# A mixture-of-experts block loop and its tail, put in another order

## The reference

```python
x = layernorm(x + dilated_attention(x))              # no weights
x = layernorm(x + cross_attention(x, ctx, Wq, Wkv, Wout))
# the part that this change touches: 32 experts, 8 of them for each of 2048 tokens
probs = softmax(x @ gate_w); w, sel = top_k(probs, 8); w = w / sum(w)
# tokens are gathered per expert (at most C = 1024 each), then per expert:
y = (silu(xg @ w_gate) * (xg @ w_up)) @ w_down       # 256 -> 96 -> 256
out[token] += w * y                                  # 8 results per token
x = layernorm(x + out)
```

## Time and profile before

| what | value |
|---|---|
| time, median of 3 runs | 707.81 us (704.06 to 709.6) |
| the profiled execution | 708.35 us, of which 706.4 us lie between its first and last instruction |
| granted clock of PE, mean over the span | 0.933 of full speed |
| busy share of the span | PE 80%, PEld 58%, POOL 55%, DVE 53%, ACT 47% |
| first stage and tables | to about 370 us |
| block loop | 377 to 645 us |
| tail | 648 to 706.4 us |

### The profile page before, as it was taken

How to read it: one execution, slowest core, us unless ns; L and a number is a source line. 1 busy time by engine, 2 the same in 40 slices (tenths; PEclk the granted TensorE clock), 3 DMA queues, 4 the chain that set the end, 5 groups by cost and what they waited for, 6 DMA issues and landing times.

```text
span 706.4 us, 17346 instructions
## 1 busy us (share of the span) xinstructions
PE 563.3 (80%) x5098; PEld 413.0 (58%) x5099; DVE 375.4 (53%) x1533; ACT 330.2 (47%) x1204; POOL 389.7 (55%) x596
## 2 busy tenths in 40 slices
PE   3768878787888778888509899989989998894995
PEld 3445444455545444554207777777877776774884
DVE  1438666667666666676333455445445544453553
ACT  2436444445554545455304555555555554553012
POOL 5353455454455655554564666666766665664532
PEclk9989999999999999999658999999999999998998
DMA  9599999821112211211235555455555554545994
GB/s 188 177 287 264 356 369 339 287 74 46 59 61 74 74 60 70 75 58 65 87 130 164 160 156 165 148 164 161 167 159 159 154 157 124 164 150 173 425 417 140
DMA packets 80540, 118.51 MB, mean 168 GB/s; under 512 B 13043, under 2 KB 70269, under 8 KB 78464
## 3 DMA queue, kind: packets, MB, share of 16 engines
q1 hardware_dynamic: 63808, 78.63, 37.0%
q0 software_dynamic: 13824, 37.78, 14.5%
q10 hardware_dynamic: 2880, 1.74, 0.8%
HBM read 56.07 MB, written 66.22 MB: 173 GB/s over the span
## 4 chain that ended last, share of the span: by engine, by line
issue 38%; PE 33%; SPq 15%; DMA 6%; POOL 2%; ACT 2%; DVE 2%; ACTq 1%; another core or an unknown queue 0%; POOLq 0%; DVEq 0%
PE bank L792 14%; PE bank L808 10%; SPq L337 8%; PE bank L784 5%; PE bank L802 3%; DMA out<-fin 3%; SPq L333 2%; DMA wall<-results 2%; SPq L332 2%; SPq L331 1%; ACTq L299 1%; ACT th L954 1%; DVE tg L1228 1%; ACT fin L983 1%; DVE hg L1231 1%
## 5 line engine op out<-in xcount | busy, mean ns | idle before, releaser
L552 POOL DMA_INDIRECT results<-ys,wcol x152 | 150.5, 990 | 25.6 <-POOL pscrap L541 19.6
L528 POOL DMA_INDIRECT queues<-x,xidx x128 | 129.4, 1011 | 37.1 <-issue 37.1
L792 PE MATMUL bank<-wall,xtT 128*128 x616 | 128.1, 331 | 1.0 <-issue 0.8
L869 ACT ACTIVATE pr<-bank,nmax 128x128 f32<-128x128 f32 x256 | 90.9, 371 | 30.1 <-DVE nmax L1021 29.7
L1228 DVE SCALAR_TENSOR_TENSOR tg<-th,bank 128x96 f32<-128x96 f32 x154 | 39.0, 253 | 116.3 <-ACT th L954 88.8
L792 PEld LDWEIGHTS bank<-wall,xtT 128*128 128x128 f32 x616 | 99.2, 195 | 2.0 <-issue 2.0
L960 ACT ACTIVATE ys<-bank,wcol 128x256 f32<-128x256 f32 x152 | 71.9, 473 | 55.6 <-PE bank L808 42.6
L808 PE MATMUL bank<-wall,hT 96*128 x304 | 95.1, 394 | 0.0
L784 PE MATMUL bank<-ident,xt 128*128 128x128 f32 x310 | 63.8, 288 | 23.4 <-DMA xt<-queues 12.1
L784 PEld LDWEIGHTS bank<-ident,xt 128*128 128x128 f32 x310 | 59.1, 198 | 38.2 <-issue 18.9
L875 ACT COPY prT<-bank 128x512 f32<-128x512 f32 x64 | 38.5, 601 | 88.5 <-PE bank L607 88.5
(11 more groups left out here) (186 smaller groups left out, 917.7 us busy)
## 6 DMA issues: line engine op xcount, KB each, us to landing
xt<-queues SPq DMA_DIRECT2D x162, 160.0 KB
results<-zeros SPq DMA_DIRECT2D x16, 1024.0 KB
wall<-results SPq DMA_DIRECT2D x16, 1024.0 KB, 13.6
queues<-zeros SPq DMA_DIRECT2D x2, 1760.0 KB
wall<-in_L_ffn_w_gate SPq DMA_DIRECT2D x4, 768.0 KB
wall<-in_L_ffn_w_up SPq DMA_DIRECT2D x4, 768.0 KB
wall<-in_L_ffn_w_down SPq DMA_DIRECT2D x4, 768.0 KB
results<-ys,wcol POOLq DMA_INDIRECT x152
```

What stands on the lines that cost most here:

```text
L528: pool.indirect_dma_start(xg, bass.IndirectOffsetOnAxis(ap=xidx[:, par, k:k + 1], axis=0), x2[:, par, :], None, bounds_check=last_row, oob ...
L552: pool.indirect_dma_start(yr, bass.IndirectOffsetOnAxis(ap=wcol[:, u, 1:2], axis=0), ys[:, u, :], None, bounds_check=last_y, oob_is_err=Fa ...
L792: ins = pe.matmul(bank[2 + u % 2][:, 0:2 * INTER].rearrange("p (g i) -> p g i", g=2), xtT[:, u % 2, kk, :], wall[:, bass.ds(e, GU)].rearrange(
L869: ins = act.activation(pr[:, g % 2, q, :], pS[g % 2][:, q * P:(q + 1) * P], ACT.Exp, bias=nmax[:, 4 * g + q:4 * g + q + 1], accum_out=den[ ...
```

## The change

Three things are put in another order, all by hand.

**The loop.** In step t PE now does the row turn of block t+5 first, then the down product of t, the turn of `hg` of t+2, and gate and up of t+4. ACT does the row copy of t+5, y of t, tanh of t+4; DVE `h_T` of t+2, `weights` of t+3, `gate` of t+4. Blocks are turned five steps ahead of their down product instead of three. Two steps more of turning and of gate and up run past the end of the list. As the second turning product of a step no longer stands behind anything that implies it, it waits by itself until ACT has read the bank that the next down product writes (`y` of block t-2).

**PE's registers.** The eight table entries per round are fetched four at a time, behind steps 1 and 5 of a round, into registers that are kept over the branch; at the end of a round eight register moves put them into place.

**The tail.** SP issues all its loads first and then its stores. A group of batches is stored by four DMAs in all, straight from a buffer for every batch (the first eight in `ys`, the others in `kP`, both free by then), so ACT waits for no earlier store. The groups are 4, 4, 4, 3 and 1.

```diff
-LEAD = UN - 2
+LEAD_G = UN
+LEAD_W = UN - 3
+LEAD_X = UN - 2
+HALF = UN // 2
-LAST = (4, 4, 4, 2, 2)
+LAST = (4, 4, 4, 3, 1)
...
+        def finished(b0, b1):
+
+            if b1 <= UN:
+                return ys[:, b0:b1, :]
+            return kP[:, :, :, :, :].rearrange("p a m q k -> p (a m q k)").rearrange(
+                "p (b d) -> p b d", d=D)[:, b0 - UN:b1 - UN, :]
...
-                eng.dma_start(out[b, t0:t0 + DIL * (GR - 1) + 1:DIL, :],
-                              fin[GR * g:GR * (g + 1), b % 4, :]).then_inc(stored[b % 4], 16)
+                eng.dma_start(out[b0:b1, t0:t0 + DIL * (GR - 1) + 1:DIL, :].rearrange("b i d -> i b d"),
+                              finished(b0, b1)[GR * g:GR * (g + 1), :, :]).then_inc(stored, 16)
...
-            for b in range(NB):
-                if b + YB < NB:
-                    sp.wait_ge(peC, b + 1)
-                    load_results(b + YB)
-                sp.wait_ge(actC, b + 1)
-                store(sp, b, 2, NG)
+            for b in range(YB, NB):
+                sp.wait_ge(peC, b - YB + 1)
+                load_results(b)
+            for n, end in zip(LAST, itertools.accumulate(LAST)):
+                sp.wait_ge(actC, end)
+                store(sp, end - n, end, 2, NG)
...
+                    if kk == 1 and not isinstance(t, int):
+                        pe.wait_ge(actF["y"], t - 4)
...
             with pe.Fori(0, rounds) as j:
-                e = neighbours(ET.PE, tab_g[0:1, bass.ds(j * UN + UN, UN)], (NE - 1) * WX)
                 for u in range(UN):
                     t = j * UN + u
-                    block_T(t + 3, u + 3, j)
-                    gu(t + 2, u, e[u])
-                    turn_h(t + 1, u + 1)
-                    down(t, u, e[u - 2] if u >= 2 else carried[u])
-                for u in range(2):
-                    pe.reg_mov(last_two[u], e[UN - 2 + u])
+                    block_T(t + 5, u + 5, j)
+                    down(t, u, down_e[u] if u < HALF else gate_e[u - HALF])
+                    turn_h(t + 2, u + 2)
+                    gu(t + 4, u + 4, gate_e[u] if u < HALF else later_e[u - HALF])
+                    if u == 1:
+                        later_e = experts_of(j * UN + (LEAD_G + UN))
+                    if u == UN - 3:
+                        coming_e = experts_of(j * UN + (LEAD_G + UN + HALF))
+                for r, v in zip(down_regs + gate_regs, later_e + coming_e):
+                    pe.reg_mov(r, v)
...
-                    block_T(t + 3, u + 3)
-                    tanh(t + 2, u)
+                    block_T(t + 5, u + 5)
                     y(t, u)
+                    tanh(t + 4, u + 4)
...
                 for i in range(n):
-                    if b >= 4:
-                        act.wait_ge(stored[b % 4], 16 * NG * (b // 4))
...
-                    act.wait_ge(actC, b)
-                    store(act, b - 1, 0, 2)
+                act.wait_ge(actC, b)
+                store(act, b - n, b, 0, 2)
...
-                columns = neighbours(ET.DVE, tab_w[0:1, bass.ds(j * UN + UN, UN)], D + NE - 1)
                 for u in range(UN):
                     t = j * UN + u
-                    weights(t + 2, u + 2, j, columns[u])
-                    gate(t + 2, u)
-                    h_T(t + 1, u + 1)
+                    h_T(t + 2, u + 2)
+                    if u == 0:
+                        columns = neighbours(ET.DVE, tab_w[0:1, bass.ds(j * UN + UN, UN)], D + NE - 1)
+                    weights(t + 3, u + 3, j, columns[u])
+                    gate(t + 4, u + 4)
```

More of the change, by code:

```diff
@@ L208, in build @@
         ys = sb("ys", [P, UN, D])
-        fin = sb("fin", [P, 4, D])
         pair_y = sb("pair_y", [P, 4, 2 * D])
@@ L260, in build @@
         y_in = [sem(f"y_in{k}") for k in range(YB)]
-        stored = [sem(f"stored{k}") for k in range(4)]
+        stored = sem("stored")
         gate_v = w_gate.rearrange("e (p k) i -> p e (k i)", k=2)
@@ L293, in neighbours, with store @@
                 skip_runtime_bounds_check_because="the tables hold rows and columns of these arrays only")[1]
-        def store(eng, b, first, last):
+        def finished(b0, b1):
[3 more added lines that the diff above has]
+                "p (b d) -> p b d", d=D)[:, b0 - UN:b1 - UN, :]
+        def store(eng, b0, b1, first, last):
             for g in range(first, last):
                 t0 = first_token(g)
-                eng.dma_start(out[b, t0:t0 + DIL * (GR - 1) + 1:DIL, :],
-                              fin[GR * g:GR * (g + 1), b % 4, :]).then_inc(stored[b % 4], 16)
+                eng.dma_start(out[b0:b1, t0:t0 + DIL * (GR - 1) + 1:DIL, :].rearrange("b i d -> i b d"),
+                              finished(b0, b1)[GR * g:GR * (g + 1), :, :]).then_inc(stored, 16)
         def combined(k):
@@ L348, in rows_of @@
                 return neighbours(ET.SP, tab_x[0:1, bass.ds(first, UN)], XG_ROWS - P)
-            first, second = rows_of(0)[LEAD:], rows_of(UN)
+            first, second = rows_of(0)[LEAD_X:], rows_of(UN)
             for k in range(2):
@@ L809, in down, with kept_registers @@
                           start=True, stop=True).then_inc(peF["y"], 1)
[L811 to L817, removed]
+            def kept_registers(name, values):
+                regs = [nc.alloc_register(ET.PE, f"{name}{k}") for k in range(HALF)]
+                for r, v in zip(regs, values):
+                    pe.reg_mov(r, v)
+                return regs, [bass.RuntimeValue.of_register_unchecked(r).with_bounds(min_val=0, max_val=(NE - 1) * WX)
+                              for r in regs]
@@ L818, in _, with experts_of @@
+            def experts_of(first):
+                return neighbours(ET.PE, tab_g[0:1, bass.ds(first, HALF)], (NE - 1) * WX)
+            down_regs, down_e = kept_registers("down_e", experts_of(LEAD_G))
+            gate_regs, gate_e = kept_registers("gate_e", experts_of(LEAD_G + HALF))
+            block_T(0, 0, 0)
+            block_T(1, 1, 0)
+            gu(0, 0, down_e[0])
+            block_T(2, 2, 0)
+            gu(1, 1, down_e[1])
+            block_T(3, 3, 0)
             turn_h(0, 0)
+            gu(2, 2, down_e[2])
@@ L965, in _ @@
                 act.copy(spare[0:1, k:k + 1], tab_n[0:1, 0:1]).then_inc(actF["y"], 1)
-            for t in range(3):
-                block_T(t, t)
-            for t in range(2):
+            block_T(0, 0)
+            for t in range(4):
+                block_T(t + 1, t + 1)
                 tanh(t, t)
@@ L1196, in tables @@
                 dve.wait_ge(s, H("fe"))
-                for tab, first, times, plus in ((tab_g, LEAD, WX, 0), (tab_w, LEAD, 1, D)):
+                for tab, first, times, plus in ((tab_g, LEAD_G, WX, 0), (tab_w, LEAD_W, 1, D)):
                     dve.tensor_scalar(tab[0:1, first:first + TAB], tab_f[0:1, 0, :], float(times), float(plus),
@@ L1237, in h_T @@
                 dve.tensor_copy(hT[:, u % 2, :], bank[4 + u % 2][0:INTER, 0:P]).then_inc(dveF["hT"], 1)
-            for t, column in zip((0, 1), neighbours(ET.DVE, tab_w[0:1, 0:UN], D + NE - 1)[LEAD:]):
+            for t, column in zip(range(3), neighbours(ET.DVE, tab_w[0:1, LEAD_W:LEAD_W + 3], D + NE - 1)):
                 weights(t, t, 0, column)
+            gate(0, 0)
+            gate(1, 1)
             for t in range(2):
-                gate(t, t)
-            h_T(0, 0)
+                h_T(t, t)
+                gate(t + 2, t + 2)
             with dve.Fori(0, rounds) as j:
-                columns = neighbours(ET.DVE, tab_w[0:1, bass.ds(j * UN + UN, UN)], D + NE - 1)
                 for u in range(UN):
                     t = j * UN + u
-                    weights(t + 2, u + 2, j, columns[u])
-                    gate(t + 2, u)
-                    h_T(t + 1, u + 1)
+                    h_T(t + 2, u + 2)
[3 more added lines that the diff above has]
+                    gate(t + 4, u + 4)
             for u in range(UN):
```

17 lines of the change are left out of this document (10 added, 7 removed).

## The result

The changed kernel takes 704.91 us in the median of 20 runs (698.83 to 709.32), the kernel before 711.12 in 20 runs (704.06 to 720.84). The ratio is 0.9917, with an interval of 0.9891 to 0.9944. So the change gains 0.8%, some 6 us; 42 were forecast, and 705 lies outside the range of 653 to 689. The profiled execution took 698.83 us, of which 697.0 lie between its first and last instruction.

A forecast was written before the change was run, and what follows sets the result against it. PE was taken to bound the loop, busy 240.0 of 268.0 us. The sum 708.35 - 22.3 (hold-ups) - 16.9 (fetches) - 2.3 (tail) = 666.9 gave a forecast of 666 us against 707.8, range 653 to 689.

The forecast's parts named there:

- So PE sets the pace: Loop: PE, busy 240.0 of 268.0 us, is the limit; 152 blocks at 1.42 are 215.8 us, 52.2 too many.
- the gain of 22.3 us from the hold-ups: Loop: 31.3 us of PE's waits (25.0 for `hg`, 6.3 short gaps) become between 0 and 14.3, 9 taken.
- I expect the late results to stay ... then costs 1.38 - 0.88: Loop: gate-and-up results still reach ACT 1.38 us late, slack becomes 0.88; 0.50 plus a 0.16 restart gap remains each time.
- the 0.66 of distance: Loop: from gate and up to the turn of `hg`, 2.07 us before and 2.73 after, so 0.66 more.
- The fetch: PE's register fetch at each round's head: 18.9 us lost before, 2 taken after, gain 16.9; four entries near 0.55 us.
- The wait for `y`: PE's wait in the loop for `y` of block t-2, issued two steps before: answered in time, so 0.
- the loads: Block loads in the loop: 8.5 us of lead against a landing of 2.1 us, so 0.
- POOL's own time: POOL in the loop: needs 1.36 us a block against PE's step of 1.42, so it isn't passed; 0.
- the filling: Filling the longer pipeline: two more turns and gate-and-ups, 1.7 us; between 0 and 1.7, 0 taken.
- The tail: After the loop: last batch's normalising starts at 700.9 instead of 703.2, gain 2.3 us, bounds 1.3 to 2.8.
- Rival 1: Loop: hold-ups keep their price, the 31.3 us stay and only heads and tail are won: 689.2 us; chance 0.17.
- Rival 3: Loop: two fetches a round hold PE 1.1 us each, 41.8 in place of 18.9, hold-ups stay: 729 us; chance 0.04.

The follow-up runs named there:

- a shorter step of PE: Changed kernel with only one of the two turning products in the loop, PE's step 0.11 us shorter: 701.39 us, ratio 0.9859.
- two pauses: Changed kernel with two more tiny POOL instructions ahead of each scatter: 693.21 us, ratio 0.9709; the same edit on the kernel before: 695.53 us, ratio 0.9759.

## Why the prediction was wrong, point by point

**"So PE sets the pace".** This is the step that failed, and with it the sum. It rested on the busy share and on waits that named PE, ACT and DVE alone. What sets the pace is how POOL's scatters follow each other. In the sum it is the gain of 22.3 us from the hold-ups that came out with the wrong sign: they cost 32 us before and 47 after (the loop above 152 undisturbed steps, without the heads), and that took back what the heads gave.

The starts of the scatters and the arrivals of PE's results, counted through the loops of four traces. A chain is three or more scatters under 1.45 us apart (the chain that ends the loop left out); a hold-up is three or more of PE's results that arrive together, each within 0.1 us of the one before:

| kernel | chains | of these, four or more scatters | hold-ups | of these, right behind a chain |
|---|---|---|---|---|
| before | 34 | 1 | 34 | 31 |
| after | 43 | 12 | 43 | 37 |
| a shorter step of PE | 41 | 17 | 39 | 34 |
| fewer rows in each scatter | 43 | 14 | 43 | 40 |

The two go together, though not one to one. The count alone does not say which brings the other, since a hold-up leaves POOL without `ys` and so ends a chain in any case. That the scatters bring the hold-ups is shown by the experiments without them, with SP's store, with every second one and with two pauses, where no result is late. In the changed kernel the results arrive 1.3 to 1.8 us after the start of the latest scatter. PE's undisturbed step of 1.42 is itself a rhythm that brings three scatters in a row too close. Then ACT and PE wait until POOL has nothing left to scatter, ACT hands over several `ys` at once, and POOL catches up at 1.36. I had that row, and read 1.36 < 1.42 as "it isn't passed", which was true of POOL's time and missed what its scatters do to PE's results.

**"I expect the late results to stay ... then costs 1.38 - 0.88".** They stayed, but neither their length nor their number was a given. The prediction made 21.6 hold-ups of one size out of 25.0 us; the trace of before has 34, of different sizes. After, there are 43, and ACT's longest wait for a gate-and-up product went from 1.8 to 3.0 (before, then after):

```profile
ACT th L954 <- PE bank L792: 39.7, 40, 1.8
```

```profile
ACT th L984 <- PE bank L802: 63.3, 54, 3.0
```

The chains got longer, too: one of four or more before, 12 after. As I read it, with more slack PE makes more blocks ahead, ACT more `ys`, and the chain lasts longer, so that the 0.66 of distance was used up by the wait it was to cover; this reading was not tested by itself.

**The fetch.** Right in itself: the heads fell from 18.9 us to 0.4. Four entries took less than the 0.55 that I put between one and eight:

```profile
L293 PEldq TENSOR_LOAD <-tab_g x40: 328/333/627, 358.4 to 634.4; - x40
```

That is also further from the 0.8, an estimate, worked out from the Trainium skill (Runtime: NRT & Kernel Launch, section Instruction fetch mechanics). That the 16.9 us of gain are real shows only without the scatter (14.9 of them); with it they are taken back, as the run with the fetches at the head shows.

**The wait for `y`, the loads, POOL's own time, the filling.** Put at 0, and none of them costs anything once the scatter is gone: the loop is then 152 steps of 1.42. With the scatter, the wait for `y` stands in the waits with 1.7 us.

**The tail.** 2.3 forecast, 2.8 to 3.0 measured; the last batch starts right at its statistics, the bound of 2.8 that I gave. Only the size was off.

**The rivals.** Rival 1 had the right word, that late results may come more often as PE waits less, and the prediction named the same as a sign that the forecast as a whole fails. Its price was too low: it left the gain of the heads standing, and that went too. Its 689 was the upper end of the range; the case in which the whole loop gain is eaten had no chance of its own but the 0.01 for no change at all. Rival 3's mechanism, fetches that hold PE, did not occur.

## What to carry to other kernels

Where results arrive late and the engines named are all idle, list what every other queue did just before, those of engines that nobody waits for first; one column of starts would have shown the scatters here. An idle time that is taken away is a gain only if what sets the rhythm is known: take the suspected cause out once (here the scatter) and see whether the floor appears. And an engine that is not the bottleneck can be made slower for a gain: scatters 1.50 and 1.64 us apart in turn, in place of 1.36, took some 3% off a kernel that had gained 0.8% by a new order.

## What was not expected of the hardware

POOL's scatters, close together, keep PE's results back. Chains of three or more, 1.36 to 1.42 us apart, go with waits of ACT for PE's results of up to 1.8 us before and 3.0 after; 2.8 apart nothing is late, nor at 1.64; at 1.50 PE still waits for `hg` up to 2.3 at a time. It is PE's results alone: where PE's turn waited for DVE's `hg`, it started at most 0.05 us after it in both kernels, and POOL at most 0.09 after ACT's `ys`; in the changed kernel a dozen of these fall in the middle of a hold-up. The loop is no shorter with 16 rows in a scatter than with 128, or with rows of 256 bytes than of 1 KB, and a store of the same bytes by SP does nothing of the kind. Not shown is what PE's results stand behind in that time, whether the product's writing is late or only the news of it (the profile models the ends of products), and whether a plain DMA started by POOL would do the same.
